# Ternary weights of the last feed-forward stage made during the second attention and kept in DRAM

## What is computed

```python
def weight_quant(w):
    scale = 1.0 / jnp.clip(jnp.mean(jnp.abs(w)), 1e-05)
    q = jnp.clip(jnp.round(w * scale), -1.0, 1.0) / scale
    return w + jax.lax.stop_gradient(q - w)

def bitlinear158(x, w, b):
    xq = act_quant(rms_norm(x))
    wq = weight_quant(w)
    return jnp.einsum('bsd,od->bso', xq, wq) + b

h = jax.nn.silu(bitlinear158(x, w1, b1))
h = jax.nn.gelu(h, approximate=False)
h = layer_norm(h, ln_g, ln_b)
return bitlinear158(h, w2, b2)
```

## Time and profile before

| | |
|---|---|
| median of three runs | 2449.18 us |
| the profiled execution | 2443.69 us |
| its span, first to last instruction | 2441.9 us |
| second attention | about 1447 to 1810 us of the span |
| long convolution | about 1813 to 2077 us |
| ternary stage | about 2080 to 2442 us |
| busy over the span | PE 77%, DVE 63%, ACT 37%, POOL 19% |

### The profile page before, as it was taken

The page is one execution under the profiler, slowest core; times in us unless marked ns, Lnnn a source line. Parts: engine busy times, 40 slices in busy tenths (PEclk is TensorE's granted clock), DMA queues, the critical chain, the costliest instruction groups (busy, mean ns, idle before and its releaser), DMA issues. The chain is left out here.

```text
span 2441.9 us, 34261 instructions
## 1 busy us (share of the span) xinstructions
PE 1885.2 (77%) x12688; PEld 1451.1 (59%) x12688; DVE 1536.7 (63%) x3007; ACT 900.1 (37%) x1525; POOL 476.0 (19%) x478
## 2 busy tenths in 40 slices
PE   3248888614376899999999959999959997178885
PEld 2225555413254799999999948877747775034442
DVE  8747776296475556665666645565635777357876
ACT  1005555500031444444444432222222002567774
POOL 0023232000001000100010001101004766024442
PEclk9859999856587999999999979999978998588897
DMA  5099999212463112222222131100032113601000
GB/s 189 0 147 142 151 150 153 81 48 77 166 207 109 52 54 75 62 68 70 77 66 71 53 107 43 36 18 27 10 107 88 44 44 132 247 0 35 27 22 22
DMA packets 149823, 199.95 MB, mean 82 GB/s; under 512 B 13472, under 2 KB 92192, under 8 KB 147232
## 3 DMA queue, kind: packets, MB, share of 16 engines
q1 hardware_dynamic: 138400, 176.84, 28.8%
q10 hardware_dynamic: 11264, 20.98, 2.3%
HBM read 151.37 MB, written 46.14 MB: 81 GB/s over the span
## 5 line engine op out<-in xcount | busy, mean ns | idle before, releaser
L453 DVE TENSOR_REDUCE a_rowmax<-a_ring 128x2 f32<-128x512 f32 x256 | 165.1, 688 | 99.8 <-PE a_ring L532 97.6
L1463 DVE TENSOR_TENSOR f_hid<-f_gate,f_gu 128x256 f32<-128x256 f32 x264 | 108.5, 420 | 163.6 <-ACT f_gate L1335 161.1
L1335 ACT ACTIVATE f_gate<-f_gu 128x256 f32<-128x256 f32 x264 | 98.7, 383 | 275.3 <-PE f_gu L1201 187.2
L2185 PE MATMUL e_py<-e_kv,e_toep 128*128 128x320 f32 x640 | 180.2, 437 | 0.0
L405 ACT ACTIVATE a_prob<-a_sT 128x1024 f32<-128x1024 f32 x128 | 130.6, 1026 | 80.2 <-PE a_sT L521 80.1
L2185 PEld LDWEIGHTS e_py<-e_kv,e_toep 128*128 128x128 f32 x640 | 119.9, 191 | 46.2 <-issue 0.8
L1214 PE MATMUL f_gu<-f_lowh,f_bg 128*128 128x256 f32 x704 | 141.2, 283 | 5.3 <-POOL f_lowl L1120 5.0
L1201 PE MATMUL f_gu<-f_xhi,f_wg 128*128 128x256 f32 x704 | 130.3, 282 | 0.0
L1201 PE MATMUL f_gu<-f_xhi,f_wu 128*128 128x256 f32 x704 | 129.1, 281 | 0.0
L1214 PEld LDWEIGHTS f_gu<-f_lowh,f_bg 128*128 128x128 f32 x704 | 115.6, 191 | 9.7 <-POOL f_lowl L1120 5.2
L1468 DVE TENSOR_TENSOR f_hl<-f_hid,f_hh 128x768 fp32r<-128x768 f32 (+2 forms) x90 | 84.5, 939 | 55.9 <-ACT f_hh L1381 54.8
(11 more groups left out here) (366 smaller groups left out, 4991.3 us busy)
## 6 DMA issues: line engine op xcount, KB each, us to landing
f_entry<-in_WdT SPq DMA_DIRECT2D x89, 256.0 KB, 2.8
a_qs<-parts SPq DMA_DIRECT2D x96, 128.0 KB, 6.4
a_ks<-parts SPq DMA_DIRECT2D x96, 128.0 KB, 7.0
parts<-a_hi SPq DMA_DIRECT2D x16, 512.0 KB, 8.7
parts<-a_lo SPq DMA_DIRECT2D x16, 512.0 KB, 9.1
e_toep<-in_taps SPq DMA_DIRECT2D x32, 256.0 KB
f_entry<-in_Bg SPq DMA_DIRECT2D x89, 64.0 KB, 1.9
f_entry<-in_Bu SPq DMA_DIRECT2D x89, 64.0 KB, 2.0
```

The lines of the kernel that those rows point to most:

```text
L453: dve.tensor_reduce(rowmax[:, s % 2, :, e * SLOTS + j], ring[n % RING][:, :].rearrange("p (q t) -> p q t", t=T), AX.X, ALU.max, negate=Tru ...
L1335: act.activation(gate[:, i % 2, :], gu[n % 3][:, 0, :], ACT.Silu).then_inc(s_["gate_ready"], 1)
L1463: dve.tensor_tensor(hid[:, j, :], gate[:, i % 2, :], gu[n % 3][:, 1, :], ALU.mult).then_inc(s_["hid_ready"], 1)
L2185: last = pe.matmul(py[n % RING][:, 0:DIAG * BS], toep[:, h % 3, (t - j) * P:(t - j + 1) * P], kv[:, h % 2, j, :], start=(j == 0), stop=(j ...
```

## The change

The sums, the means, the scaling, the clamping and the rounding leave the ternary stage. They are done in the second attention, in its two `staging` slots, one piece of 128 x 2048 values at a time, each matrix in four pieces:

- In steps 0, 1 and 2 ACT sums the magnitudes of the eight pieces, at three places of its step: after the second exponential, after the last feature copy, and after the copies of the turned input. SP loads pieces between, each when its slot is free.
- In step 3 POOL adds the sums over the partitions, for both matrices at once, before its other work of the step, and DVE makes the two means and inverses between the second rows of values and the last `feature_low`.
- SP loads the eight pieces a second time. In steps 3 to 6 ACT scales two of them a step, at the second and third place.
- In steps 4 to 7 POOL clamps and rounds two pieces each, at the start of its step, ahead of its additions and roots, into two bfloat16 slots; SP stores them in a DRAM tensor `ternary` and then loads the next piece into the slot that is free.
- The ternary stage loads the four bfloat16 pieces of w1 before the gain, shift and b2 rows, and those of w2 behind them. All its own making of weights is gone; the inverse means stay in two small tiles that are held from one stage to the other. SiLU of the first three tiles waits for its product alone.

```diff
+SCRATCH |= {"ternary": ([2 * KT, P, INNER], BF16)}
...
+    PIECES = 2 * KT
+    SUMMED = {(0, 0): 0, (0, 1): 1, (0, 2): 2, (1, 0): 3, (1, 1): 4, (1, 2): 5, (2, 0): 6, (2, 1): 7}
+    MEANS_IN, SCALE_IN = 3, 3
...
+        wraw = staging[:, :, :, :].rearrange("p n k o -> p n (k o)")
...
+                def load_piece(m):
+
+                    if m < 2:
+                        sp.wait_ge(s_["w_split"], m + 3)
+                    elif m < PIECES + 2:
+                        sp.wait_ge(s_["wsum_ready"], m - 1)
+                    else:
+                        sp.wait_ge(s_["w_ready"], m - PIECES - 1)
+                    k = m % KT
+                    if m % PIECES < KT:
+                        sp.dma_start(wraw[:, m % 2, :], io["w1"][k * P:(k + 1) * P, :]).then_inc(got_w[m % 2], 16)
...
+                def send_piece(c):
+                    sp.wait_ge(s_["w_ready"], c + 1)
+                    sp.dma_start(io["ternary"][c], wq[:, c % 2, :]).then_inc(sent_w[c % 2], 16)
...
                 for b in range(1, XT):
                     load_x(b)
+                load_piece(0)
+                load_piece(1)
                 for b in range(B):
+                    if b <= 2:
+                        for m in range(3 * b + 2, min(3 * b + 5, PIECES + 2)):
+                            load_piece(m)
+                    if b > SCALE_IN:
+                        for c in (2 * (b - SCALE_IN) - 2, 2 * (b - SCALE_IN) - 1):
+                            send_piece(c)
+                            if c + 2 < PIECES:
+                                load_piece(PIECES + c + 2)
                     sp.wait_ge(s_["x_ready"], (b + 1) * TB)
...
                 for step in STEPS:
+                    if step == MEANS_IN:
+                        pool.wait_ge(s_["wsum_ready"], PIECES)
+                        pool.partition_all_reduce(wall[:, :], wsum[:, :], P, bass.bass_isa.ReduceOp.add).then_inc(s_["wall_ready"], 1)
+                    if step > SCALE_IN:
+                        for c in (2 * (step - SCALE_IN) - 2, 2 * (step - SCALE_IN) - 1):
+                            pool.wait_ge(s_["w_scaled"], c + 1)
+                            pool.tensor_scalar(wraw[:, c % 2, :], wraw[:, c % 2, :], -1.0, 1.0, ALU.max, ALU.min
+                                               ).then_inc(s_["w_clamped"], 1)
+                            pool.wait_ge(s_["w_clamped"], c + 1)
+                            if c >= 2:
+                                pool.wait_ge(sent_w[c % 2], 16 * (c // 2))
+                            pool.tensor_scalar(wq[:, c % 2, :], wraw[:, c % 2, :], ROUND, -ROUND, ALU.add, ALU.add
+                                               ).then_inc(s_["w_ready"], 1)
                     b = step + 1
...
+                def magnitudes(step, place):
+                    if (step, place) in SUMMED:
+                        c = SUMMED[step, place]
+                        act.wait_ge(got_w[c % 2], 16 * (c // 2 + 1))
+                        if c >= 2:
+                            act.wait_ge(s_["wsum_ready"], c - 1)
+                        act.activation(wq[:, c % 2, :], wraw[:, c % 2, :], ACT.Abs, accum_out=wsum[:, c:c + 1]
+                                       ).then_inc(s_["wsum_ready"], 1)
+
+                def scale_piece(c):
+                    act.wait_ge(s_["winv_ready"], 2)
+                    act.wait_ge(got_w[c % 2], 16 * (PIECES // 2 + c // 2 + 1))
+                    act.activation(wraw[:, c % 2, :], wraw[:, c % 2, :], ACT.Identity, scale=winv[:, c // KT:c // KT + 1]
+                                   ).then_inc(s_["w_scaled"], 1)
...
                             if pr >= 2:
                                 feature_high(step, pr - 2)
+                            if pr == 1:
+                                magnitudes(step, 0)
                     if now:
                         feature_high(step, PR - 2)
                         feature_high(step, PR - 1)
+                        magnitudes(step, 1)
+                        if SCALE_IN <= step < SCALE_IN + KT:
+                            scale_piece(2 * (step - SCALE_IN))
...
+                    magnitudes(step, 2)
+                    if SCALE_IN <= step < SCALE_IN + KT:
+                        scale_piece(2 * (step - SCALE_IN) + 1)
...
                         value_rows(step + 1, 1)
+                    if step == MEANS_IN:
+                        dve.wait_ge(s_["wall_ready"], 1)
+                        for n in range(2):
+                            mean = wmean[:, n:n + 1]
+                            wm.step(dve.tensor_reduce(mean, wall[:, n * KT:(n + 1) * KT], AX.X, ALU.add))
+                            wm.step(dve.tensor_scalar(mean, mean, 1.0 / (D * INNER), 1e-5, ALU.mult, ALU.max))
+                            dve.reciprocal(winv[:, n:n + 1], mean).then_inc(s_["winv_ready"], 1)
                     if now:
                         feature_low(step, PR - 1)
...
@@ the ternary stage @@
-                for k in range(KT):
-                    sp.dma_start(pieces[k], io["w1"][k * P:(k + 1) * P, :]).then_inc(got_w[k], 16)
                 for t in range(2):
                     sp.dma_start(xt[:, t, :], io["x5"][t * P:(t + 1) * P, :]).then_inc(got_x[t], 16)
                 sp.dma_start(b1[:, :], io["b1"].broadcast_to([P, INNER])).then_inc(s_["rows_in"], 16)
                 for k in range(KT):
-                    sp.dma_start(pieces[KT + k].rearrange("p (j o) -> p j o", o=D),
-                                 io["w2"].rearrange("(k j p) o -> k p j o", p=P, k=KT)[k]).then_inc(got_w[KT + k], 16)
+                    sp.dma_start(w1[:, k, :], io["ternary"][k]).then_inc(s_["got_w1"], 16)
                 for dst, name in ((gain, "lng"), (shift, "lnb"), (b2, "b2")):
                     sp.dma_start(dst[:, :], io[name].broadcast_to([P, dst.shape[1]])).then_inc(s_["rows_in"], 16)
+                for k in range(KT):
+                    sp.dma_start(w2[:, k * 4:(k + 1) * 4, :], io["ternary"][KT + k].rearrange("p (j o) -> p j o", o=D)
+                                 ).then_inc(s_["got_w2"], 16)
...
-                for n in range(2):
-                    pool.wait_ge(s_["wsum_ready"], (n + 1) * KT)
-                    pool.partition_all_reduce(wall[:, n * KT:(n + 1) * KT], wsum[:, n * KT:(n + 1) * KT], P, bass.bass_isa.ReduceOp.add
-                                              ).then_inc(s_["wall_ready"], 1)
                 pool.wait_ge(s_["rows_in"], 64)
...
-                magnitudes(0)
-                scaled(0)
-                magnitudes(1)
 
                 def silu(t):
                     act.wait_ge(s_["h_done"], t + 1)
-                    if t < 3:
-                        act.wait_ge(s_["w_ready"], 2 * KT)
-                    else:
+                    if t >= 3:
                         act.wait_ge(s_["gained"], t - 2)
...
-                    if s == 1:
-                        scaled(1)
...
-                            pe.wait_ge(s_["w_ready"], KT)
+                            pe.wait_ge(s_["got_w1"], 16 * KT)
...
-                            pe.wait_ge(s_["w_ready"], 2 * KT)
+                            pe.wait_ge(s_["got_w2"], 16 * KT)
...
-                ternary(0)
+                dve.tensor_scalar(wfac[:, :], winv[:, 0:1], 127.0, None, ALU.mult).then_inc(s_["wfac_ready"], 1)
                 dve.wait_ge(s_["wfac_ready"], 1)
...
-                        if t == 1:
-                            ternary(1)
```

More of the change, by code:

```diff
@@ L1594, in attention1 @@
     STEPS = range(-2, B)
+    PIECES = 2 * KT
+    SUMMED = {(0, 0): 0, (0, 1): 1, (0, 2): 2, (1, 0): 3, (1, 1): 4, (1, 2): 5, (2, 0): 6, (2, 1): 7}
+    MEANS_IN, SCALE_IN = 3, 3
+    held = ExitStack()
+    fix = Maker(nc, held)
+    wmean, winv = fix.sb("g_wmean", [P, 2]), fix.sb("g_winv", [P, 2])
+    keep["ternary"] = dict(held=held, wmean=wmean, winv=winv)
     SCALE = G ** -0.5
@@ L1635, in attention1 @@
         stats = mk.sb("d_stats", [P, B, TB, 10])
+        wq = mk.sb("d_wq", [P, 2, INNER], BF16)
+        wsum = mk.sb("d_wsum", [P, PIECES])
+        wall = mk.sb("d_wall", [P, PIECES])
         ring = [mk.ps(f"d_ring{n}", [P, 512]) for n in range(RING)]
@@ L1645, in attention1 @@
         stored = [sem(f"d_stored{u}") for u in range(XT)]
+        got_w = [sem(f"d_got_w{u}") for u in range(2)]
+        sent_w = [sem(f"d_sent_w{u}") for u in range(2)]
+        wraw = staging[:, :, :, :].rearrange("p n k o -> p n (k o)")
         with nc.Block() as block:
@@ L1675, in _ @@
                     sp.wait_ge(stored[u], 16 * (B // XT))
+                for u in range(2):
+                    sp.wait_ge(sent_w[u], 16 * KT)
             @block.gpsimd
@@ L1937, in normal @@
                                       ).then_inc(s_["x_ready"], 1)
-                av, tail = Chain(dve, s_["av_steps"]), Chain(dve, s_["tail_steps"])
+                av, tail, wm = (Chain(dve, s_[n]) for n in ("av_steps", "tail_steps", "wmean_steps"))
                 dve.memset(ones[:, :], 1.0).then_inc(s_["made"], 1)
```

(41 more changed lines are left out.)

13 lines of the change are left out of this document (6 added, 7 removed).

## The result

The changed kernel takes 2437.93 us (median of 6 runs, 2432.75 to 2441.35), the kernel before in the same series 2449.2. The ratio is 0.9953, 95% interval 0.9938 to 0.9967: 11.3 us faster, where I had forecast 27, and 0.9 us above the range that I gave. The profiled execution took 2438.21 us.

The account below looks back on a forecast made before the run. PE bounds the second attention; the ternary opening's chain of waits (root, SiLU 0) lies on the path. Gains of 28.1 us less 1.1 for DVE's means give -27.0: 2449.18 to 2422.2 us, own range 2418 to 2427, 8-in-10 range 2418 to 2437.

Parts of the forecast that it names:

- POOL in the attention: Second attention: sixteen POOL sweeps of 1.8 us (upper bound 4.7), four a step, hidden in POOL's idle time; cost 0.
- the step on DVE: Second attention: two means cost 1.1 us once; layer norm's last step may wait 0.8 to 3.7 us more, cost 0.
- Rival C: Attention steps 4 to 7: every POOL sweep holds DVE up, unabsorbed, 3.2 to 14.8 us; 2425.4 to 2437.0 us; chance 0.10.
- Rival D: Attention steps 4 to 7: far dearer sweeps make POOL's roots late; slower kernel above 9.0 us a sweep; chance 0.04.
- signs of being wrong: Attention step growing over 2 us, ACT waiting for a DMA at a third place, root still 7 us behind b2's landing.
- The root: Ternary opening: POOL's first root at about 2097.3 instead of 2120.64, about 17 us behind the stage's start; gain 23.3 us.
- The 7.08 us of reload: Ternary opening: the delay from b2's landing to the first root is POOL's reload and goes with the change.
- rival B: Ternary opening: queues don't serve in order, root waits for all 9.25 MB; 9.6 us later, 2431.8 us; chance 0.07.
- SiLU 0: Ternary opening: SiLU of tile 0 starts 0.1 us behind its product, no longer waiting for w2; gain 4.8 us.
- The two means: Second attention: six DVE instructions before the last `feature_low` and the maxima, charged in full once; cost 1.1 us.
- ACT's sums and scales: Second attention: eight sums of 1.91 us and eight scalings of 1.99 fit ACT's idle times; cost 0.
- The reloads in step 3: Second attention: the sum over partitions brings two POOL reloads of 9.0 us each, 18 in all, hidden.

Follow-up runs that it names:

- quarters: Changed kernel with each POOL sweep cut into four of 512 columns, everything computed: 2423.25 us, one run.
- cheap form: Changed kernel with all sixteen sweeps as multiply by 1.0 and add 0.0 over 2048 columns, clamping and rounding left out: 2416.84 us, ratio 0.9881.
- first trace: Profiled execution of the changed kernel, nothing further altered: 2438.21 us, attention 389.4 us.
- second trace: The changed kernel run once more, unaltered, for another trace: 2435.03 us, attention 387.4 us.
- first pair: First traces of the kernel before and the changed kernel: ternary stage 361.7 and 331.2 us; second traces of both: 359.3 and 330.8 us.
- the run of the forms: Changed kernel with other operations and sizes in the places of single POOL sweeps, so weights are not ternary: 2424.32 us, one run.

## Why the prediction was right in part and wrong in sum

The step that failed is the one on POOL in the attention: "I take 1.8, since a sweep has one tensor input as the cast has", with the bounds 1.8 and 4.7 and "Cost 0 by either bound". Measured: 7.1 us. The upper bound was no bound, because it came from another instruction with other arithmetic. By itself that length would still have been hidden in steps 4 to 6 (quarters: 41.5 us a step with POOL busy for longer), but not in the last step: four sweeps are 28.5 us there, ahead of roots that came after 22.9.

The second failure stands in the step on DVE: a wait of "0.8 to 3.7 us more ... so 0". I looked for one held instruction, the layer norm's, and priced that. It was held by 6.9 us and DVE caught up in steps 4 to 6, as I said. The instruction that costs is `feature_low`, which reads two tensors, both in SBUF, and which PE waits for through the values and maxima behind it. I never listed which of DVE's instructions fall into the time of the sweeps. By step, second root to second root, against 41.5, 41.5, 41.5, 40.3, 26.8 before:

| step | 3 | 4 | 5 | 6 | 7 |
|---|---|---|---|---|---|
| after | 42.3 | 44.6 | 44.5 | 44.9 | 37.7 |
| quarters | 42.3 | 41.5 | 41.5 | 40.3 | 34.8 |
| cheap form | 42.3 | 41.5 | 41.5 | 40.3 | 26.7 |

Rival C was the right mechanism ("every sweep holds DVE up, and nothing absorbs it"), with its time of 2425.4 to 2437.0 too low by its sweep's price, and the place was another: 3 us a step in steps 4 to 6 (4.5 in step 6 of the first trace, 3.0 of the second), and 10.9 in the last step. That the measured 2437.93 lies next to its 2437.0 is luck: its 14.8 us stand against some 22 measured, and gains elsewhere that were larger than forecast make up for it. Rival D had the last step's place, a POOL that comes late: it isn't what happened in the change, where the roots wait for DVE by 5.01 us, but it is what is left once DVE is free (quarters, 8 us). Its condition for a late step 7, four sweeps over 22.9 us, was met at T = 7.1; that for a slower kernel, T above 9.0, was not.

Of the signs of being wrong that I named, two came: steps longer by over 2 us, and ACT waiting for a load at the third place (step 6, 4.06 us, in the second trace 4.57). The third, 7 us between b2 and the root, did not.

The other steps, one by one:

- The root: forecast 17 us after the stage's start, measured 19.6 (2124.72 - 2105.12); gain 20.8 against 23.3. The 7.08 us of reload went as forecast. b2 was late: the windows of 4 us from the stage's start (last column GB/s) give 6.9 million bytes up to its landing, and what was asked for up to b2 is 6.0. So some 0.9 million bytes of what was asked for later came ahead of it, about 2 us: rival B in small. No run tested this apart.

```profile
2105.12:2109.12 4.00, 0.00 (x0) 0.00 (x0) 0.84 (x3) 0.72 (x2) 0.00 (x0) 0.50 0.64 231
2109.12:2113.12 4.00, 0.00 (x0) 0.00 (x0) 0.00 (x0) 0.00 (x0) 0.00 (x0) 0.50 0.99 340
2113.12:2117.12 4.00, 0.00 (x0) 0.00 (x0) 0.00 (x0) 0.00 (x0) 0.00 (x0) 0.50 1.03 416
2117.12:2121.12 4.00, 0.00 (x0) 0.00 (x0) 0.00 (x0) 0.00 (x0) 0.00 (x0) 0.50 1.01 423
2121.12:2125.12 4.00, 0.00 (x0) 0.00 (x0) 0.00 (x0) 0.00 (x0) 0.32 (x2) 0.50 1.02 352
```

- SiLU 0: forecast 4.8, measured 5.9 (its activation follows the root by 2136.59 - 2124.72 = 11.87 us; before by 17.75, from 2120.64 to 2138.39). I had kept the table load (1.28 us) on the path; without the wait for w2, ACT loads it while PE multiplies.
- The product of tile 1: not in my sum. Its bias products take 3.67 us instead of 5.13, at a granted clock of 1.00 instead of 0.71. Ahead of it PE had stood idle for 6.11 us while DVE made w2; in the changed kernel it is idle there for 1.71 us. 1.5 us.
- The two means: forecast 1.1, step 3 is longer by 0.8 in every trace with the change.
- ACT's sums and scales: 0, as forecast. The one wait of ACT for a load (4.06 us, step 6) held nothing up: behind it ACT waits 8.04 us for PE.
- The reloads in step 3: 5.80 and 7.00 us of idle time in place of 9.0 each, hidden. The Trainium skill (GPSIMD Engine Reference, 2.1 Instruction dispatch) has about 6 us for the first call after a load; the 5.80 agree, the 7.00 and the 9.0 of the old opening are longer.
- The rest of the ternary gain (2.3 us in the first pair, 0.3 in the second) is within the spread of that stage.

## What to carry to other kernels

Before work goes to an "idle" engine, price the very form of instruction, with its operations, in the trace or by a run of its own; a neighbour with the same inputs was wrong by four times. Then list the instructions that an engine which it can hold (here DVE) runs during that time, and mark those that read SBUF alone and that the bounding engine waits for: here those that read PSUM kept their time. If they can't be avoided, cut the long instruction, move it behind the latency-bound work of a short last step (not tried here), or give it to an engine with idle time that holds nobody here: two activations of 2 us on ACT did what two sweeps of 7 us did on POOL.

## What the runs showed of the hardware

- POOL's `tensor_scalar` over 128x2048 float32: 7.14 us for maximum and minimum or for two additions, 5.37 for one maximum, one addition or one multiplication (5.39), 1.90 for multiply and add. Adding a second operation, multiply and add against multiply alone, made it 2.8 times faster. Maximum, addition and multiplication alone were measured once each.
- DVE isn't held for the whole sweep in each case. `feature_low` ended 4.77 to 4.79 us after the start of a sweep of 7.1 us each time it was fully held (five times in the first trace), and one that started 5.98 us behind the sweep's start took its usual 0.42. The layer norm's step, `tensor_scalar`, was held to the end of the sweep of 2048 columns, although it starts 0.05 us ahead of it in the trace. The Trainium skill (SBUF — State Buffer, Who interferes with whom) says that an instruction with two SBUF inputs contends with a POOL instruction that reads SBUF, and that where one is in a two-port mode the first of the two has the shared ports for its whole length and the other waits. Two kinds of hold are in the trace too; that the first ends at a fixed point inside the sweep would fit an end of POOL's reads at about 4.36 us (4.78 less the instruction's own 0.42), an estimate that no run here tests.
- The hold falls faster than the length. In the run of the forms (timeline below), beside a sweep over 1024 columns of 3.64 us, the layer norm's step took 1.37 us, so it was held for 0.8, not 3.6; in the quarters, beside 512 columns of 1.9 us, it took 0.94 us. Beside 2048 columns in the cheap form, also of 1.9 us, it took 2.23 to 2.25, so it isn't the length alone.

```profile
1749.59 1.37 DVE L2048 TENSOR_SCALAR d_xt<-d_xt,d_stats 128x512 f32<-128x512 f32 x1 [0.67 <-POOL d_stats L1784]
1749.64 3.64 POOL L1746 TENSOR_SCALAR d_staging<-d_staging 128x1024 f32<-128x1024 f32 x1
```

Why 1024 and 512 columns hold DVE so much less than 2048 is open.
